# Four column tiles for the weighting, a detour through DRAM and three moved jobs in an attention and expert kernel

## The reference

```python
x = x + attention(layernorm(x))   # 16 heads of 8; q, k = low-rank part + rotary part
x = x + experts(layernorm(x))     # 24 experts, the 2 best of each token
# attention of one batch and head:
p   = softmax(query @ key.T / sqrt(144))
out = p @ value                    # then out @ Wo + bo
# expert e: gelu(x @ w1[e] + b1[e]) @ w2[e] + b2[e], weighed by the softmax of the two best scores
```

## Time and profile before

| | |
|---|---|
| median of 3 runs | 682.04 us (681.6 to 684.51) |
| profiled execution, its own time | 684.42 us |
| span of its trace | 682.6 us |
| busy in the span | PE 83%, PEld 60%, DVE 71%, ACT 54%, POOL 47% |
| mean granted TensorE clock | 0.92 |
| pass 2 of the first head of batch 0 starts | 44.46 us |
| first expert matmul | 475.2 us |

### The profile page before, as it was taken

How to read it: one execution, slowest core, us unless ns; L and a number is a source line. 1 busy time by engine, 2 the same in 40 slices (tenths; PEclk the granted TensorE clock), 3 DMA queues, 4 the chain that set the end, 5 groups by cost and what they waited for, 6 DMA issues and landing times.

```text
span 682.6 us, 16712 instructions
## 1 busy us (share of the span) xinstructions
PE 566.9 (83%) x4218; PEld 412.4 (60%) x4219; DVE 484.1 (71%) x1485; ACT 371.0 (54%) x933; POOL 323.2 (47%) x374
## 2 busy tenths in 40 slices
PE   3478999898998998998999989812999999999910
PEld 2335565565555555555555545411999999999910
DVE  7677888788998998998997958542555555555536
ACT  1215765665764764764764746611555555555532
POOL 5531446445445445445446414442455655656622
PEclk9869999799998998998998959965999999999975
DMA  6343423323333333332343421485322222222055
GB/s 215 73 112 84 130 77 101 107 72 102 101 91 92 97 97 86 99 99 82 101 114 97 138 78 42 163 286 187 77 62 61 62 62 61 62 64 64 8 175 194
DMA packets 54482, 69.52 MB, mean 102 GB/s; under 512 B 7026, under 2 KB 42107, under 8 KB 53808
## 3 DMA queue, kind: packets, MB, share of 16 engines
q1 hardware_dynamic: 47856, 58.14, 29.5%
q0 software_dynamic: 4864, 8.54, 3.8%
q10 hardware_dynamic: 1728, 2.43, 1.0%
HBM read 46.85 MB, written 23.41 MB: 103 GB/s over the span
## 4 chain that ended last, share of the span: by engine, by line
PE 53%; issue 14%; DVE 14%; POOL 9%; DMA 4%; ACT 2%; SPq 2%; DVEq 1%; POOLq 0%; ACTq 0%
PE s L681 12%; PE s L689 11%; PE pv L524 10%; PE s L492 5%; DVE mx L846 4%; POOL dispatched L1322 4%; PE s L511 4%; PE pb L544 2%; DVE w L1230 2%; PE pb L545 2%; PE pm L501 1%; PE pb L675 1%; PE pb L539 1%; SPq L359 1%; DVE mrest L859 1%
## 5 line engine op out<-in xcount | busy, mean ns | idle before, releaser
L846 DVE TENSOR_REDUCE mx<-s 128x2 f32<-128x512 f32 x256 | 170.9, 684 | 44.1 <-PE s L492 43.1
L714 ACT ACTIVATE pr<-s 128x512 f32<-128x512 f32 x256 | 147.9, 592 | 93.1 <-PE s L511 91.2
L825 ACT ACTIVATE pr<-s,wts 128x128 f32<-128x128 f32 x352 | 100.6, 368 | 85.3 <-PE s L681 85.3
L524 PE MATMUL pv<-pr,vm 128*64 128x256 f32 x1024 | 144.5, 405 | 0.0
L1384 POOL DMA_INDIRECT results<-pr,ridx x88 | 100.8, 1146 | 83.8 <-DVE pr L1198 54.6
L492 PE MATMUL s<-w 72*128 72x256 bf16 x512 | 103.7, 286 | 7.5 <-DVE mx L846 7.0
L511 PE MATMUL s<-w 75*128 75x256 bf16 x512 | 101.7, 281 | 4.8 <-ACT pr L714 2.4
L681 PE MATMUL s<-turn,vm 128*128 128x128 f32 x704 | 96.5, 281 | 0.0
L689 PE MATMUL s<-w,pr 128*128 x704 | 93.2, 275 | 0.6 <-ACT pr L825 0.5
L1322 POOL DMA_INDIRECT dispatched<-pay,pos x64 | 63.5, 992 | 55.2 <-DVE pos L1006 20.9
L524 PEld LDWEIGHTS pv<-pr,vm 128*64 128x64 f32 x1024 | 64.0, 140 | 41.3 <-issue 17.9
(11 more groups left out here) (150 smaller groups left out, 770.8 us busy)
## 6 DMA issues: line engine op xcount, KB each, us to landing
w<-parts_out SPq DMA_DIRECT2D x32, 288.0 KB
w<-parts_out SPq DMA_DIRECT2D x96, 96.0 KB
w<-in_w SPq DMA_DIRECT2D x16, 512.0 KB, 3.8
parts_out<-qkp SPq DMA_DIRECT2D x16, 384.0 KB, 2.8
tin<-dispatched SPq DMA_DIRECT2D x88, 66.0 KB, 1.8
w<-in_w SPq DMA_DIRECT2D x4, 1024.0 KB, 6.4
w<-results SPq DMA_DIRECT2D x8, 512.0 KB, 7.5
dispatched<-qkp SPq DMA_DIRECT2D x12, 198.0 KB, 2.1
```

Of the source, the lines that this page charges most:

```text
L524: mm = nc.tensor.matmul(pv[2 * QW * c:2 * QW * (c + 1), r, :], vm[s][:, t, 2 * r + c, 2 * QW * i:2 * QW * (i + 1)], pr[h // NG % 2][:, h % ...
L714: nc.scalar.activation(pr[h // NG % 2][:, h % NG, :, :], s2[h % 2][:, :, :], ACT.Exp, scale=SCALE).then_inc(exp_done, 1)
L825: last = nc.scalar.activation(hT[t.pair][:, c, :], hps[t.pair][:, :, :].rearrange("p a s -> p (a s)")[:, c * P:(c + 1) * P], ACT.Gelu, bia ...
L846: nc.vector.tensor_reduce(mx[j % 2][:, :, g], s1[h % 2][:, :, :], AX.X, ALU.max).then_inc(max_done, 1)
```

## The change

- `weigh` takes one quarter's four heads and one half of the keys per call: four matmuls with 32 columns each (one of ones, eight of values, else zeros), in four column tiles of 32. Calls stand at (q, 1) and (q, 3) for q of 1 to 3; both calls for the last quarter stand at (0, 1) of the next step. There are eight calls of four matmuls, as before.
- The eight ACT copies go. SP stores the copied tile to DRAM (`store_weighed`) and loads sums (each row to eight partitions) and values from there (`load_weighed`). ACT's `take_weighted` moves to (0, 2), the reciprocals to (2, 0) and (2, 1).
- The split of the maxima goes from DVE to POOL, with four places in POOL's order. `leave` goes from DVE to POOL.
- Pass 1 runs three quarters ahead instead of two, the turn two instead of one; the split still lies between a quarter's last maximum and the turn at (q, 1) of the quarter after.
- Both LayerNorms are applied on ACT, one activation with scale and bias for 128 tokens: `normalise_x` at (0, 0), `normalise_rows` at (3, 2), which writes both copies of a row at once. POOL makes the bias (`shift1`, `shift2`, two small operations each).
- Values are copied by ACT (`take_values`, at (1, 3) before `second_part`); their bias goes, through one matmul in the prologue, into the output bias. `first_part` moves to (1, 0), `take_maxima` to (q, 2).
- Two of the four copies of w1 of the experts get SBUF of their own.

```diff
+            def store_weighed(b):
+                done, read = known_count(sp, b + 1), known_count(sp, b * 16)
+                wait(sp, pv_done, done)
...
+                sp.dma_start(weighed_out.rearrange("r p s -> p r s"), weighed_sb[:, :, :]).then_inc(weighed_st, 16)
+            def load_weighed(b):
+                stores, used = known_count(sp, (b + 1) * 16), known_count(sp, b)
+                wait(sp, weighed_st, stores)
+                wait(sp, norm_st, used)
...
+                sp.dma_start(sums[:, :], rows_out[:, None, 0:S].broadcast_to([H, HD, S])).then_inc(sums_in, 16)
+                sp.dma_start(outT[:, :], rows_out[:, S:(HD + 1) * S]).then_inc(nums_in, 16)
...
+            def weigh(b, s, j, t):
+                r, i = divmod(j, 2)
...
+                wait(pe, exp_done, b * H + NG * (j + 1))
+                for c in range(NG):
+                    mm = nc.tensor.matmul(pv[VW * c:VW * (c + 1), r, :], vm[s][:, t, (r * NG + c) * 2 + i, :],
+                                          pr[j % 2][:, c, t, :],
                                          start=(i == 0 and t == 0), stop=(i == 1 and t == QT - 1), skip_group_check=True)
                mm.then_inc(pv_full, 2)
-                    if held.attend if q < 2 else held.lead:
+                    if leads(held, q):
...
+                    if q == 0 and g == 1 and held.route:
+                        for t in range(QT):
+                            weigh(b - 1, 1 - s, NQ - 1, t)
+                    if q > 0 and g % 2 == 1 and held.attend:
+                        weigh(b, s, q - 1, g // 2)
...
+                    if held.route and (q, g) == (3, 2):
+                        normalise_rows(b - 1)
...
                         elif (q, g) == (1, 3):
+                            take_values(b + 2)
                             second_part(b + 2)
+            def normalise_rows(b):
+                wait_apart(act, sent, b * (QT * TOPK * 16))
+                wait_apart(act, shift_st, (b + 1) * 2)
+                for t in range(QT):
+                    last = nc.scalar.activation(pay[:, t, :, 0:D], x_all[:, bass.ds(b * QT + t, 1), :].broadcast_to([P, TOPK, D]),
+                                                ACT.Identity, bias=shift2[:, t:t + 1], scale=rstd2[:, t:t + 1])
...
+            def split_maxima(m, j):
...
+                nc.gpsimd.tensor_copy(xp[:, :, 0, :], x).then_inc(split_st, 1)
+                nc.gpsimd.tensor_tensor(mrest[:, :, :], x, xp[:, :, 0, :], ALU.subtract).then_inc(split_st, 1)
+                nc.gpsimd.tensor_tensor(xp[:, :, 1, :], x, xp[:, :, 0, :], ALU.subtract).then_inc(split_st, 1)
+                nc.gpsimd.tensor_tensor(xp[:, :, 2, :], mrest[:, :, :], xp[:, :, 1, :], ALU.subtract).then_inc(split_done, 1)
...
+                if held.attend:
+                    split_maxima(*turning(b, s, 0)[::2])
                 if held.project:
                     sum_turns(b + 2)
                 if held.lead:
                     give_values(b + 1, 1 - s)
-                if held.prepare:
-                    normalise_x(b + 3)
+                if held.attend:
+                    split_maxima(*turning(b, s, 1)[::2])
                 if held.project:
+                    leave(b + 2)
                     third_part(b + 2)
+                if held.lead:
+                    split_maxima(*turning(b, s, 2)[::2])
                 if held.send:
                     send(b - 2, s)
                 if held.project:
                     add_out_bias(b + 2)
+                if held.lead:
+                    split_maxima(*turning(b, s, 3)[::2])
                 if held.route:
                     deviation_rows(b - 1)
-                    normalise_rows(b - 1)
-                    twin_rows(b - 1)
                 if held.prepare:
                     add_biases(b + 3)
```

More of the change, by code:

```diff
@@ L411, in step @@
             def step(b, s):
                 held = Held(b)
[L413 to L433, removed]
@@ new lines, in step @@
+                known = isinstance(b, int)
+                if held.lead and not (known and b == 0):
+                    spread_rows(b + 1, 1 - s, 1)
+                if held.route:
+                    store_weighed(b - 1)
+                if held.attend:
+                    add_maxima(*turning(b, s, 0))
+                if held.route:
+                    load_weighed(b - 1)
+                if held.attend:
+                    add_maxima(*turning(b, s, 1))
+                if held.project and not (known and b < 2):
+                    e = (b - 2) * (NE // (NB - 4))
+                    sp.dma_start(w1[:, bass.ds(e, NE // (NB - 4)), 0:DF], w1v[:, bass.ds(e, NE // (NB - 4)), :]).then_inc(ld_w1, 16)
@@ L442, in _ @@
             add_maxima(0, 0, 0)
-            for half in range(2):
-                spread_rows(1, 1, half)
+            spread_rows(1, 1, 0)
+            add_maxima(0, 0, 1)
+            spread_rows(1, 1, 1)
             pipeline(sp, step)
@@ L597, in step @@
                         pass2(b, s, h)
-                    if g == 1 and (held.lead if q == NQ - 1 else held.attend):
+                    if g == 1 and turns(held, q):
                         turn_max(*turning(b, s, q))
@@ L770, in step @@
                     q, g = divmod(h, NG)
-                    if g == 1 and (held.lead if q == NQ - 1 else held.attend):
+                    if g == 2 and turns(held, q):
                         m, _, j = turning(b, s, q)
@@ L1028, in step @@
                         stats_x((10 + 3 * q) * QT, (13 + 3 * q) * QT)
-                    if held.project and (q, g) == (1, 2):
-                        leave(b + 2)
                     if held.project and (q, g) == (1, 0):
@@ L1139, in _ @@
             take_qk(0, lead_banks[2])
-            dve.wait_ge(ld_r, 16)
-            take_values(0)
-            leave(0)
             stats_x(4 * QT, 10 * QT)
@@ L1146, in _ @@
             take_qk(1, lead_banks[2])
-            take_values(1)
-            leave(1)
             normalise_x(2)
+            dve.wait_ge(ld_r, 16)
+            dve.wait_ge(obias_full, 1)
+            nc.vector.tensor_tensor(brow[:, R_O:R_O + D], pb[:, 0:D], brow[:, R_O:R_O + D], ALU.add).then_inc(obias_st, 1)
             take_rotary(2, r1_full, turn1, C_COS, r1_done, True, pb)
-            for g in range(NG):
-                maximum(0, 0, 0, g)
-            split_maxima(0, 0)
-            for g in range(NG):
-                maximum(0, 0, 1, g)
-            split_maxima(0, 1)
+            for j in range(NQ - 1):
+                for g in range(NG):
+                    maximum(0, 0, j, g)
             pipeline(dve, step)
@@ L1370, in _ @@
                     deviation_x(2 * QT, 4 * QT, 2)
+                leave(m)
                 third_part(m)
@@ L1373, in _ @@
                     give_values(0, 0)
+            deviation_x(4 * QT, 10 * QT, 4)
             add_biases(2)
-            deviation_x(4 * QT, 10 * QT, 4)
+            pool.wait_ge(obias_st, 1)
+            for m in range(2):
+                add_out_bias(m)
+            for j in range(2):
+                split_maxima(0, j)
             pool.wait_ge(ld_x, 32)
```

260 lines of the change are left out of this document (123 added, 137 removed).

## The result

The changed kernel takes 710.87 us (median of 4 runs, 704.88 to 712.84), the kernel before 682.17 beside it: ratio 1.0399, 95% interval 1.0332 to 1.0466. It is slower, as forecast, but by 28 us and not by 8, and outside the range of 674 to 706. Some executions on the chip fall into a slower state; ratios leave them out, medians do not.

A forecast was written before the change was run, and what follows sets the result against it. PE bounds the loop with DVE close behind; after the change POOL closes the ring. Loop +4.7, first batches -3.7, batches 13 to 15 -1.9, tail +9: +8.1 on 684.42, 692.5, as median 690 us; range 674 to 706.

The forecast's parts named there:

- A to T1: Loop, from pass 2 of head 7 at (1, 3) to the turn at (2, 1): 4.15 us, -0.1 a batch.
- T1 to T2: Loop, turn at (2, 1) to turn at (3, 1), waiting for POOL's send, bias and split: 7.8 us, +1.5 a batch.
- T2 to A: Loop, turn at (3, 1) to the next pass 2 of head 7, PE setting the pace: 12.8 us, -2.15 a batch.
- POOL's ring: Loop: POOL's chain closes the ring, so PE's 3.7 us a batch are not gained; batch 24.75 against 25.52 before clock cost.
- Outside the loop: Step pricing the first two batches at -3.7, batches 13 to 15 at -1.9, prologue at 0, tail at +9 us.
- Batches 0 and 1, -3.7: Start, where no send stands on POOL: 4.15 + 4.6 + 12.7 against 3.6 + 5.45 + 14.4, about -2 us each.
- Batches 13 to 15, -1.9: End of the loop: fewer waits and shorter calls of `weigh`, -1.9 us in all.
- The tail, +9: After W, the last weighing: ACT's 12 paddings wait behind `normalise_rows` of batch 15; +9 us, bounds +4 and +11.
- The held clock: Rival for the loop: clock holds or half stretches fall where POOL's chain hides them; 677 us, faster; chance 0.22.
- The paddings did come late: Tail rival said the opposite: paddings not late, ACT's queue reaching them before the normalising; 681 us, no change; chance 0.10.
- Four tiles that run as two pairs: Rival on `weigh`: four tiles run as two pairs, five calls between turn (3, 1) and pass 2 keep 0.43; 718 us; 0.06.
- DVE and POOL do hold each other up: Rival: the two block each other at memory, one `normalise_out` of 0.4 us before the turn at (2, 1); 695 us; 0.07.

The follow-up runs named there:

- the kernel with filled turns: Changed kernel plus unread matmuls into unused PSUM columns, 24 ahead of the turn at (2, 1) and 40 ahead of (3, 1): 693.05 us, ratio 1.0144.
- The two splits on DVE alone: Changed kernel with only the splits turned at (2, 1) and (3, 1) back on DVE, the other two on POOL: 687.57 us, ratio 0.9991.
- the last kernel: Changed kernel with two splits on DVE, paddings and power moved, turns and tail filled, w2 loads behind SP's paddings: 659.86 us, ratio 0.9691.

## Why the prediction was wrong

**Right: the loop.** Each cut came as worked out: A to T1 3.99 (4.15), T1 to T2 7.65 to 7.69 (7.8), T2 to A 13.93 (14.0 with the clock's share), a batch 25.60 (25.95). The split takes 0.96, the call of `weigh` lost 0.44 (0.43). The Trainium skill, page "TensorE: Matmul & The Clock Gate", section on packing small matmuls, has a figure for three column tiles, from which the prediction estimated a loss of 0.32; the measurement stands nearer to four tiles at full overlap. PE's gain went where it was said to go, into POOL's ring, which the kernel with the splits on DVE shows by undoing it. A stretch of half clock after a stall was the right mechanism; the 1.2 us a batch were 0.8. On eleven batches this and the cuts make +0.9 of the +4.7 forecast, so the loop, which the forecast had as half of its loss, is nearly level. One mark was off: a wait of over 2.5 us at (3, 1) shows in two of the eleven batches (0.45 at 248.70), because PE comes there late, at half clock; in the kernel with filled turns 40 matmuls of 2.40 us and a wait of 0.79 stand in that place, 3.2 as worked out.

**Wrong: the step "Outside the loop", -3.7, -1.9 and +9.** These sum to +3.4; measured are +27.5, with 0.3 in the prologue, put at 0. Against the forecast of +8.1 the start is 11.4 us worse, batches 13 to 15 are 6.0, the tail 4.5, the experts 1.8 and the prologue 0.3, and the loop is 3.8 better: that is the way to 28.4. That the direction came right is in part luck: 3.8 of the forecast 8.1 us were not there, and losses that nobody had forecast stood in their place.

- Batches 0 and 1, -3.7, were +7.7. The stall on the third part's chain was in the sum (A to T1 4.15, measured 3.98). Left out were the half clock behind it, which I priced in the loop only, and the power of twelve columns ahead of a split. T1 to T2, put at 4.6, took 6.98 and 7.44 with no wait at T2, and T2 to A of batch 0, put at 12.7, took 17.57 with the stall of 3.33 in it. The two splits on DVE alone bring these batches to 43.4, 2.0 below before. How much of the rest is clock stays open: with the filling they still take 51.7, but there the stall at 72.45 is not filled, and the 40 matmuls stand on PE's own way, T1 to T2 taking 6.35 and 6.80 with no wait at T2.
- Batches 13 to 15, -1.9, were +4.1. Of batches 13 and 14 the clock took 6.0 (48.3 with, 42.3 without). Up to W the timeline points to the trip through DRAM: in the short slots of step 15 the output projection comes at 445.00, after a wait of 3.63, for sums whose load went out at 438.51. I had called the trip hidden in the loop and put no price on it in these batches. No run isolates it.
- The tail, +9, was +13.5. The mechanism, ACT's paddings behind its LayerNorm, was the right one, and the size was off: product at W + 12.45 and not at 9.0, since both calls ran at half clock (1.94 for 1.1) and the load of the sums took 5.0 us to the reciprocals where store and load were put at 5.0 together. Moving the paddings brings back 6.2 of the 13.5. In what is left stand w2's loads and SP's paddings, which I had not looked at and which the trip pushed behind W. Moving w2's loads brought the send 5.5 us forward and the experts 1.6; the last kernel is still 6.2 us over the gap of before, and that rest was not taken apart.
- The experts, put at nothing, were +1.8. Half of the first-layer weights now lie outside `vm`, and their copies take 0.54 us for 0.50. But the stretch is 207.4 us in the run that only moves the power, and 207.4 to 210.2 over all traces of the changed kernel and its variants, so the 1.8 us may be no cost of the change at all.

**The rivals.** The held clock would have been 677 by my count; held by filling it was 693, so that rival's error is that of the same step. The paddings did come late. Four tiles that run as two pairs are out, with a call of 0.57 us. DVE and POOL do hold each other up, but at DVE's split operations, which the change had taken away: POOL's took 0.20 to 0.21 us in the mean and never over 0.30 in the changed kernel.

## What to carry to other kernels

A relief of the busiest engine is worth what the next queue allows: time each turn through every engine's own order, at the start and the end of the loop as well as in it, because the steady batch, on which I spent the working, moved by 0.1 us here, and 27.5 of the 28.4 us came in 5 batches out of 16, the tail and what lies around them. Price a stall of TensorE with the half clock that follows it, and test it by filling the idle place with matmuls that nothing reads: this also tells what the clock hides, here that two kernels 13 us apart at the last weighing were within 3 us of each other. At the end of a loop list what each DMA queue still has to issue, since a transfer that the loop hides stands bare there and pushes back what is queued behind it.

## What was not expected of the hardware

- Matmuls that do no work made both kernels faster: the changed one from a ratio of 1.0399 to 1.0144, the one before by 0.8% (0.4 to 1.2).
- With the splits on DVE, a cast of 128x8 elements took 0.17 us alone and 0.65 in the mean when an operation of POOL was under way; 32 of these 37 ended 0.02 to 0.04 us after one.
- The same 128x256 load of the sums out of DRAM was 3.5 us from issue to use in step 15 and 5.0 in the tail, where loads of w2 were issued 1.2 us behind it; with these moved away it was 3.9 and 4.1. The spread is wide: with the loads behind it the other traces have 4.3 to 5.5.
